# Second key sort of a graph kernel: the mask compare takes its upper operand from PSUM

## The reference

```python
edge_index = jnp.stack([src, dst])
x = _layernorm(x + _L0_gnn_ref(x, edge_attr_2, src, dst, ...))      # softmax over the edges of each dst
x = _layernorm(x + _L1_gnn_ref(x, edge_index))                      # sum over the edges of each dst
x = _layernorm(x + _L2_gnn_ref(x, edge_index, edge_attr_16, ...))   # softmax over the edges of each src
x = _layernorm(x + _L3_gnn_ref(x, src, dst, ...))                   # softmax over the edges of each dst
```

## Time and profile before

| | |
|---|---|
| median of 3 runs | 11699.41 us (11692.87 to 11706.48) |
| profiled execution | 11700.35 us, span 11698.6 us |
| mean granted TensorE clock | 0.572 |
| busy in the span: POOL, DVE, ACT, PE | 71%, 48%, 23%, 21% |
| busy with the gathers of the second block (L625, 1504 of them) | 1611.0 us |
| compares of the second sort (L369), 128x1024 and 128x512 forms | 115.9 us and 91.6 us |

### The profile page before, as it was taken

How to read it: one execution, slowest core, us unless ns; L and a number is a source line. 1 busy time by engine, 2 the same in 40 slices (tenths; PEclk the granted TensorE clock), 3 DMA queues, 4 the chain that set the end, 5 groups by cost and what they waited for, 6 DMA issues and landing times. The chain is left out here.

```text
span 11698.6 us, 56700 instructions
## 1 busy us (share of the span) xinstructions
PE 2434.3 (21%) x11904; PEld 1961.6 (17%) x11904; DVE 5630.7 (48%) x13767; ACT 2651.5 (23%) x3853; POOL 8344.7 (71%) x8546
## 2 busy tenths in 40 slices
PE   2322434322000000000000000666666530000000
PEld 2211323222000000000000000555555420000000
DVE  9999898971422222411111112777777642222223
ACT  0155545540211111112222210111111231111111
POOL 0077777777777777777777777777777667777776
PEclk8555555555555555555555555888888765555555
DMA  7011111011222222222222222333333212222222
GB/s 224 11 13 12 14 13 14 7 28 34 63 54 56 56 55 55 50 52 53 52 53 53 53 50 45 85 87 87 87 87 87 63 32 55 55 54 54 55 55 49
DMA packets 689050, 631.38 MB, mean 54 GB/s; under 512 B 453790, under 2 KB 511799, under 8 KB 687681
## 3 DMA queue, kind: packets, MB, share of 16 engines
q0 software_dynamic: 273056, 240.52, 13.7%
q1 hardware_dynamic: 414782, 380.93, 10.1%
q10 hardware_dynamic: 864, 6.29, 0.1%
HBM read 322.29 MB, written 304.83 MB: 54 GB/s over the span
## 5 line engine op out<-in xcount | busy, mean ns | idle before, releaser
L1223 POOL DMA_INDIRECT l_rows<-table,l_sources x4704 | 4466.6, 950 | 1463.4 <-issue 1432.8
L625 POOL DMA_INDIRECT e_rows<-in_rec,base x1504 | 1611.0, 1071 | 1056.1 <-DVE marks L754 605.1
L1223 POOL DMA_INDIRECT l_pair<-table,l_slab x1568 | 1506.8, 961 | 483.3 <-issue 457.1
L1425 DVE TENSOR_TENSOR_SCAN l_totals<-l_factor,banks 128x510 f32<-128x510 f32 (+3 forms) x672 | 752.7, 1162 | 1672.3 <-ACT banks L1580 1671.1
L1590 ACT COPY l_kept<-l_totals 128x476 f32<-128x476 f32 (+3 forms) x672 | 638.9, 967 | 3184.5 <-DVE l_totals L1425 3174.9
L1356 DVE TENSOR_TENSOR l_score<-l_rows,base 128x14 f32<-128x14 f32 x224 | 43.4, 194 | 2662.8 <-DMA l_rows<-table,l_sources 2662.8
L1542 PE MATMUL banks<-ident,l_kept 128*65 128x128 f32 (+2 forms) x4 | 1.9, 463 | 5854.0 <-DVE junk L1474 5854.0
L1542 PEld LDWEIGHTS banks<-ident,l_kept 128*65 128x65 f32 (+2 forms) x4 | 0.7, 170 | 5856.1 <-DVE junk L1474 5856.1
L772 PE MATMUL banks<-marks 125*128 125x98 bf16 x3200 | 623.0, 366 | 1237.1 <-DVE marks L754 1237.1
L390 DVE COPY_PREDICATED area<-banks,area 128x2048 f32<-128x2048 int32 x342 | 869.2, 2598 | 0.2
L1532 PE MATMUL banks<-w_each,l_turned 128*128 128x288 f32 (+1 forms) x1344 | 658.2, 578 | 167.6 <-ACT l_turned L1612 167.6
(11 more groups left out here) (312 smaller groups left out, 6091.8 us busy)
## 6 DMA issues: line engine op xcount, KB each, us to landing
l_rows<-table,l_sources POOLq DMA_INDIRECT x4704, 2.5
sums<-l_kept SPq DMA_DIRECT2D x112, 476.0 KB, 3.0
sums<-l_kept SPq DMA_DIRECT2D x224, 231.0 KB, 3.5
sums<-l_kept SPq DMA_DIRECT2D x112, 462.0 KB, 2.6
seeds<-late_rows SPq DMA_DIRECT2D x130, 392.0 KB
sums<-l_kept SPq DMA_DIRECT2D x112, 448.0 KB, 2.5
l_pair<-seeds SPq DMA_DIRECT2D x224, 224.0 KB, 3.4
l_pair<-table,l_slab POOLq DMA_INDIRECT x1568, 2.5
```

The costliest lines, as they stand in the source:

```text
L625: GP.indirect_dma_start(e_rows[:, u, g, :], None, A["rec16"], bass.IndirectOffsetOnAxis(e_ids[:, s * G16 + g:s * G16 + g + 1], 0)).then_in ...
L1223: GP.indirect_dma_start(pair[:, u, g, 0:D] if gated else rows[:, u, g, :], None, table[l], bass.IndirectOffsetOnAxis(at, 0)).then_inc(rows ...
L1425: V.tensor_tensor_scan(flat(totals[:, s % 2, h, 0:n, :]), flat(factor[:, s % 2, 0:n, :]), flat(fresh[s % 2][h][:, 0:n, :]), 0.0, ALU.mult, ...
```

## The change

In every stage of the second sort but the 7 flipped ones, ACT first copies the upper key halves (`[:, :, 1, :]`, 128 x 1024 fp32) into `swap`, the PSUM banks of the mask, and counts on `copied`. DVE waits for that count, and its compare reads the lower halves from SBUF and the upper ones from `swap`, which it overwrites with the mask in the same instruction. The waits behind it count one copy more per stage. The first sort does not take this path.

```diff
         def copies_until(n):
 
-            return sum(2 + (not (in_rows(e["j"]) and e["j"] == e["k"] - 1)) for e in PLAN[:n])
+            return sum(2 + 2 * (not (in_rows(e["j"]) and e["j"] == e["k"] - 1)) for e in PLAN[:n])
 
@@ sort_vector
                 ins, outs = pairs(a, k, j), pairs(b, k, j)
+                if by_mask:
+                    dve.wait_ge(s["copied"], copies_until(n) + 1)
                 if loads:
                     for (lo, hi, up), m in zip(ins, swap_views(k, j)):
                         if flipped:
                             ins_m = V.scalar_tensor_tensor(m, hi, -1.0, lo, ALU.mult, ALU.is_lt if up else ALU.is_gt)
                         else:
-                            ins_m = V.tensor_tensor(m, lo, hi, ALU.is_gt if up else ALU.is_lt)
+                            ins_m = V.tensor_tensor(m, lo, m.bitcast(F32), ALU.is_gt if up else ALU.is_lt)
@@ sort_vector
                     if by_mask:
-                        dve.wait_ge(s["copied"], copies_until(n) + 1)
+                        dve.wait_ge(s["copied"], copies_until(n) + 2)
@@ sort_scalar
                     if not (in_rows(j) and j == k - 1):
+                        low = 1 << address_bit(j)
+                        AC.copy(swap.bitcast(F32).rearrange("p (x l) -> p x l", l=low),
+                                key[e["side"]].rearrange("p (x j l) -> p x j l", j=2, l=low)[:, :, 1, :]
+                                ).then_inc(s["copied"], 1)
                         AC.copy(key[1 - e["side"]][:], key[e["side"]][:]).then_inc(s["copied"], 1)
```

## The result

| | before | after |
|---|---|---|
| median | 11699.41 us | 11643.26 us (11638.78 to 11650.94, 5 runs) |
| profiled execution, span | 11700.35, 11698.6 us | 11643.26, 11641.5 us |
| ratio to before | | 0.9951 (95%: 0.9940 to 0.9961) |
| last gather of the second block ends | 2815.1 us | 2762.5 us |
| DVE's sort and decode end | 2585.4 us | 2630.6 us |

The change gains 0.5%, 56 us by the medians.

The account below looks back on a forecast made before the run. POOL's gathers were taken to bound the block: -81.9 + 3.7 + 12.1 = -66 us against 11700.35, or -73 followed from the first gather. The middle, -70, gave 11630 us, range 11608 to 11656.

Parts of the forecast that it names:

- What bounds the kernel: End of the second block: POOL's last gather at 2815.1 us sets it, DVE's sort has 230 us to spare.
- The hold goes in full with the second SBUF input: Gathers under the compare L369 from 1201 us on: 97 held for 81.9 us, all taken as gone.
- The rival that it stays: Compare with one PSUM input holds POOL as before; only costs left, +12 to +13 us, 11713 us; chance 0.06.
- the rule that the Trainium skill marks as inferred: By it the compare has no hold to remove and the change only costs; same time as the staying hold, 11713 us.
- Length of the compare: DVE's compare with an input in PSUM stays unchanged at 1.23 us, or 0.70 for the halves.
- the rivals that need a longer one: Compare twice as long without a hold, 11698 us, chance 0.04; compare longer and still holding, up to 11876, chance 0.03.
- The 62 cycles: Fixed cost the skill adds for a PSUM source, 0.065 us a compare by estimate; the prediction's rows showed none.
- ACT's copy: Copy into PSUM takes 1.03 us, hidden in stages with a histogram step; elsewhere DVE's L384 starts 0.93 us later.
- What reaches POOL: Up to 1201 us nothing gained, 13 exposed stages cost 12.1 us; behind it POOL gains every hold.
- The sum of the holds: Gathers from 1201 us on: 81.9 us of compare holds gone, 3.7 us added under other instructions.
- The walk down the rows: Following gathers one by one over DVE's rows: remaining holds rise from 69.7 to 73.4 us.
- None of the rivals: Hold stays (chance 0.06), compare twice as long (0.04), ACT's copy slow (0.06), compare both holds and is longer (0.03).

Follow-up runs that it names:

- every kernel of the table: The kernel before, the changed kernel and six follow-up kernels run beside the same kernel before; medians from 11556.99 to 11720.34 us.
- the slower chips' kernels: On chips 14% slower: kernel before with memsets behind both histogram instructions, 1.0001 and 1.0010 of before; kernels without POOL's wait for the histogram, 1.0707 to 1.0841.
- the costs alone: The changed kernel with the compare reading both halves from SBUF again, ACT's extra copy and DVE's wait kept; 11720.34 us, 1.0020 of before.
- The late part alone: The kernel before with the change only from stage 63 on, behind POOL's last long stand-still; 11637.43 us, 0.9942 of before.
- the early part alone: The kernel before with the change only in the first 63 stages; 11717.73 us, 1.0015 of before.
- The spacers, e4: Change from stage 63 on, plus a one-element memset between the two histogram instructions from step 74 on; 11610.20 us, 0.9923 of before.
- the counts in PSUM: The kernel before with the histogram's constant input read from PSUM in the second block, compare unchanged; 11594.23 us, 0.9907 of before.
- the kernel with both: The change from stage 63 on together with the histogram's constant input in PSUM; 11556.99 us, 0.9876 of before.
- e2: The kernel before with the change only from stage 63 on; 11637.43 us, 0.9942 of before.
- e10, e13: A run on the chips where the kernel before took 14% more; the text given does not say which kernel has this number, nor its time.

## Why the prediction was right, and where it was off

The forecast was 11630 us in a range of 11608 to 11656, the median is 11643: right in sign, cause and range, with four fifths of the forecast gain.

- *What bounds the kernel.* Right. POOL ends the block in every kernel of the table, and its last gather moves with the time. In the slower chips' kernels, which are not in it, DVE ends it.
- *The hold goes in full with the second SBUF input.* Right: of 128 gathers under the compare one is longer, by 0.22 us. The gathers that start under L1403 and L384 are 227 and 349 by the trace, not 396 and 311, but as the prediction says none of them is held. The rival that it stays is what the costs alone look like, and they were run: 11720, not 11643. Forecast for that case was 11713. With it fell the rule that the Trainium skill marks as inferred ("SBUF — State Buffer", Who interferes with whom), that `tensor_tensor` does not stall software DMAs, as far as these gathers go. In the first kernel 124 of 127 gathers under L369 were held. The other rule of that section, that an instruction with at most one SBUF input and outside the 2-port modes does not contend, was borne out twice, by L371 and by L772.
- *Length of the compare.* Right, 1.229 us in place of 1.233, so the rivals that need a longer one fell. The 62 cycles, by estimate 0.065 us, that the Trainium skill's table ("VectorE: DVE Perf Modes", The TRN2 errata) adds for a PSUM source did not show.
- *ACT's copy.* 1.025 us for a forecast of 1.03, hidden in the stages with a histogram step. In the others L386 starts 2.98 us behind the stage's start instead of 2.00, a cost of 0.98 for 0.93. DVE's end moves by 45 us, forecast 41.
- *What reaches POOL.* Right in kind: the stand-still at 1200.98 moved to 1214.94, 14.0 us for 12.1. The late part alone removes that shift, and the early part alone gains nothing.
- *The sum of the holds* is the term that was off. It said 81.9 us off and 3.7 on, so 78.2; measured are 150.8 less 84.3, 66.5. The step that failed is the reading "the gather is held until the instruction under which it starts ends". Where two holding instructions follow each other without a gap, POOL may miss its turn. Of the 81.9 us booked to L369 some 15 belonged to gathers that an L754 had caught, such as the one of 3.81 us; with the compare out of the way gathers of this kind still wait through both L754. The walk down the rows found 73 us left where there are 84. The spacers and the counts in PSUM show it.
- *What is left.* 66.5 less 14.0 is 52.5, the whole shift of the last gather (52.6). So the two terms that were measured worse than forecast, the holds by 11.7 us and the stand-still by 1.9, make the sum -52.5 where the prediction's own was -66, and -70 after it took the middle. Some us either way are chance: the same instructions, started 14 us later in the early part, gave 8 us more of holds. So part of how near the forecast came is luck.

None of the rivals had part in the outcome.

## What to carry to other kernels

Where POOL issues indirect DMAs all the time, count DVE's instructions with two SBUF inputs beside it: each holds the gather that starts under it, and one input in PSUM sets that gather free; here DVE's instruction took no longer for it. Look also at one-input instructions that go at double rate (below). Ask first on whose pace POOL goes in that stretch, since a hold taken away while it waits for somebody is only a longer wait, and put the extra copy where it is hidden. When a delay is booked to what ended last, look at what it began under: of several causes in a row, the last one gets the blame, and its removal gives back only its own part.

## What the runs showed of the hardware

- A gather of POOL (DMA_INDIRECT, 0.94 us) that starts under a DVE `tensor_tensor` with two SBUF inputs ends 0.81 us after that instruction. With one input in PSUM it is let through: 1 of 128 takes longer under the compare (by 0.22 us), and 1 of 259 under the histogram's in the kernel with both (by 0.61 us, with L359, a TENSOR_SCALAR, starting 0.18 us into it).
- Two SBUF inputs are not the only case. L355, a TENSOR_SCALAR that runs once a block, has one such input and a column of signs, and goes through 2048 fp32 elements in 1.27 us where the compare needs 1.23 for 1024. In the kernel before, the changed one, e2 and e4 the gather that starts under it is held too, and ends 0.81 or 0.82 us after it:

```profile
1105.07 1.27 DVE L355 TENSOR_SCALAR area<-area,sign 128x2048 f32<-128x2048 f32 x1
1105.39 1.77 POOL L625 DMA_INDIRECT e_rows<-in_rec,base  x1 [0.30 <-DVE marks L754]
```

- Two holding DVE instructions back to back, the second starting 0.08 us before the first has ended, can keep POOL out through both (2.63 us), three through all three (3.81 us). With a memset of one element, 0.06 us, put between them in the program, 16 holds of over 1.25 us became 2.
- `tensor_tensor` on bf16 keeps its rate of 2048 elements in 1.215 us with one input in PSUM, and a compare that overwrites the PSUM words that it reads takes 1.229 us for 1024 fp32, as from SBUF (1.233).
- On two chips, where the kernel before took 14% more, DVE makes 38 instructions in 200 us (1000 to 1200 us, e10 and e13) beside unbroken indirect DMAs of POOL instead of 120, and the profile shows hardly anything that it waits for. The cause is open.
